# Four units of key and value projection moved ahead of the first attention step, and the rest planned anew

## The chip, the cores and the metric

The kernel runs on one core of one Trainium2 chip. The metric is the time of one execution on the device in microseconds (us). Engines are called PE (matrix products), DVE (vector), ACT (activation), POOL (general) and SP (which here only issues DMAs).

## What is computed

A cross attention over 16 heads of 32 channels, then a feed-forward block. All 1600 query tokens attend to all 5776 context rows. Cut to the part that the change touches:

```python
q = (x @ Wq + bq).reshape(1, B * N, H, hd)          # x: layernorm of (16, 100, 512), H = 16, hd = 32
kv = (cond @ Wkv + bkv).reshape(1, -1, 2, H, hd)    # cond: (16, 361, 512)
k, v = (kv[:, :, 0], kv[:, :, 1])
q, k = _fq_sym(q * scale, axis=-1), _fq_sym(k, axis=-1)   # 8-bit steps, one scale for each row and head
v = _fq_sym(v, axis=2)                                    # one scale for each channel, over all rows
attn = _fq_unsigned(softmax(einsum('bhqd,bhkd->bhqk', q, k)), axis=-1)
out = einsum('bhqk,bhkd->bhqd', attn, v)
```

## The kernel before, in words

The context rows are cut into NU = 46 tiles of 128 rows. The heads are taken in NG = 4 groups of four. One **unit** (g, u) projects context tile u onto the keys and the values of head group g: `unit` on PE (lines 562 to 587; eight fp32 products and a bias product for it, in four slices), `unit_out` on ACT (lines 804 to 818; a key half and a value half, PSUM to SBUF, which counts up `s_kve`), and `load_unit` on SP (line 324), which loads the context tile into one of RING = 4 buffers CT and first waits until PE has done the unit four before it (`s_ku`). Four units are a batch: DVE reduces it (`batch`), ACT rounds it one step later (`k_round`) and splits it two steps later (`k_high`), POOL does `k_scale` and `k_parts`, SP stores it three steps later (`store_k`).

The **first stage** runs all 46 units of group 0, with the query tiles between them: 9 behind the first nine batches, and tiles 9 to 12 behind the last. Then ACT turns all values of group 0 into integers (`value_ints`, three parts, lines 855 to 863), and SP transposes them in the DMA engines (lines 477 to 481).

The **attention loop** has NA = 200 steps. A step is one tile of 128 query rows of one head against all keys: PE makes the scores in four chunks (`scores`, line 637) into two PSUM buffers PS that take turns; DVE scales each chunk and keeps its least value (line 1119), and closes the step with line 1141; ACT takes the exponential of the step (line 946); SP transposes its result by DMA (line 522); POOL widens it (`unpack`, line 1368); PE multiplies it by the values four steps later (`values`, line 656), and ACT takes that product out (`values_out`, line 902). The DMA issues of a step, its transposes with them, all stand in SP's one queue: tiles CT, stores of key batches, stores of finished heads (`store_out`, at step 7 of each 25), the key pieces of the next head (`load_head`, at 1, 3, 5, 6, 8, 15, 16, 18, 20 and 22 of each 25), then the transpose.

The units of groups 1 to 3 are woven into these steps. `plan_units` (lines 98 to 106) gives each its step: a group starts seven steps after the end of the one before, and has one unit in each step, with two in the step in which u // 6 (group 1) or u // 16 (groups 2 and 3) grows. `UNITS` is the same table by step. A unit's four slices stand on PE behind the four chunks of scores and values; `unit_out` stands on ACT one step ahead in its loop, between the exponential and `values_out`. The attention loop on PE thus begins with the first chunk of scores of step 0 and a slice of unit (1, 0) behind it, at a point where ACT is at `value_ints`.

Of the kernel before, what the change touches and what calls it, by code (L numbers as in the profile page):

```python
# [44 lines left out]
NT = -(-TOK // P)  # L45
LAST = TOK - (NT - 1) * P
FULL = NT - 1
NU = -(-KEYS // P)
# [12 lines left out]
VT_LO = (0, 16, 32)  # L61
# [10 lines left out]
NB = 4  # L72
# [25 lines left out]
def plan_units():  # L98


    steps, start = {}, 0
    for g in range(1, NG):
        for u in range(NU):
            steps[g, u] = start + u - (u // 16 if g > 1 else u // 6)
        start = steps[g, NU - 1] + 7
    return steps

# [2 lines left out]
UNITS = {}  # L110
# [31 lines left out]
def build(nc, x, ctxt, ctxl, Wq, bq, Wkv, bkv, Wp, bp, w13T, w2T, norm_w, eye, Qd, Kd, Od, Rd, out):  # L142
    ctx = ExitStack()
    with ctx:
# [132 lines left out]
        M = {n: sem(n) for n in names}  # L277
# [46 lines left out]
        def _(sp):  # L324
# [100 lines left out]
                                   Qd[0:Q_HEAD * P, 0, :]).then_inc(M["s_q0"], 16)  # L425
            store_k(0, NBT - 3)
            load_wg(1)
            for s in range(3):
                for g, u in UNITS[s]:
                    load_unit(g, u)  # L430
            store_k(0, NBT - 2)
            store_q(Q_HEAD)
            load_head(0, 3)
# [48 lines left out]
            sp.wait_ge(M["s_qd0"], 16 * (-(-NT // 2)))  # L482
            sp.wait_ge(M["s_qd1"], 16 * (NT // 2))
            load_head(0, 0)
            for i in range(NA):
                p, j = divmod(i, PAIRT)
                for g, u in UNITS.get(i + 3, []):
# [39 lines left out]
            for s in range(NT + 3):  # L527
                if s < NT:
                    n = rows(s)
# [14 lines left out]
                if 0 <= s - 1 < NT:  # L544
                    t = s - 1
                    n = rows(t)
# [4 lines left out]
                if 0 <= s - 3 < NT:  # L551
                    t = s - 3
                    n = rows(t)
# [7 lines left out]
        def _(pe):  # L561
# [47 lines left out]
            for b in range(NBT):  # L609
                for u in BATCH[b]:  # L610
                    unit(0, u)
                if b == 0:
                    pe.wait_ge(M["s_bk"], 16 * 2)
                    x_transpose(0)
                for t in Q_AFTER[b]:
                    query(t)
                    if t + 1 < NT:
                        x_transpose(t + 1)
            def scores(i, c):

                n = NC_ * i + c
                _, segs = tile_of(i)
                if c == 0:
                    for h, *_r in segs:
                        pe.wait_ge(s_kt[h % 3], 16 * NC_ * (h // 3 + 1))
                        if h == 0 and i < Q_HEAD:
                            pe.wait_ge(M["s_q0"], 16)
                        else:
                            pe.wait_ge(s_qt[h % 3], 16 * (h // 3 + 1))
                if n == 1:  # L630
                    pe.wait_ge(M["s_qe"], NT)
                if n >= 2:
                    pe.wait_ge(M["s_ev"], n - 1)
                for f in range(0, CW[c], 512):
                    w = min(512, CW[c] - f)
                    for h, q0, r, p0 in segs:
                        last = pe.matmul(PS[n % 2][p0:p0 + r, f:f + w], QT[h % 3][0:PARTS * HD, q0:q0 + r],  # L637
                                         KT[h % 3][0:PARTS * HD, c * CHUNK + f:c * CHUNK + f + w],
                                         start=True, stop=True)
                last.then_inc(M["s_qk"], 1)  # L640

            def values(i, part):

                _, segs = tile_of(i)
                g = i // PHASE
# [3 lines left out]
                if part == 0:  # L649
                    if i % PHASE == 0:  # L650
                        for r in range(VRING if g else 0):
                            pe.wait_ge(s_vb[r], 16 * (NBT * g // VRING))
                        pe.wait_ge(M["s_vi"], 16 * len(VT_LO))
                    pe.wait_ge(*((M["s_pve"], i) if i else (M["s_kve"], NU)))
                for u in range(*PV_PART[part:part + 2]):
                    last = pe.matmul(PO[:, 0:w], PT[i % 2][:, u, :].bitcast(F16),  # L656
                                     VI[g % 2][:, u, h * HD:h * HD + w], start=(u == 0), stop=(u == NU - 1))
# [144 lines left out]
        def _(act):  # L802
# [118 lines left out]
                    act.wait_ge(M[f"r_st{t % 2}"], 16 * (t // 2))  # L921
                act.activation(XO[t % 2][0:n, :], PK[0:n, :], ACT.Copy).then_inc(M["r_xo"], 1)

            for u in UNITS[0]:
                unit_out(*u)
            def transposed(t):
                act.wait_ge(M["f_tp"], t + 1)
# [10 lines left out]
            for i in range(NA):  # L938
                act.wait_ge(M["s_mx"], i + 1)
                if i < 2:  # L940
                    act.wait_ge(M["s_pad"], i + 1)
                if i == 0:
                    act.wait_ge(M["s_vt"], len(VT_LO))
                if i >= 2:
                    act.wait_ge(s_tr[i % 2], 16 * (i // 2))
                act.activation(Pr[i % 2].rearrange("p t q b -> p t b q"),  # L946
# [513 lines left out]
```

## Time and profile before

| | us |
|---|---|
| median of 3 runs | 1908.86 |
| lowest and highest of them | 1904.17, 1917.34 |
| the profiled execution | 1917.34 |
| its span in the trace | 1915.5 |

The profiled execution is the slowest of the three; 1.84 us of its time lie outside the span. All durations below are from it. A view of windows gives, for each stretch, its length, the busy time and count of each engine, the granted clock of PE as a share of 2.4 GHz, the DMA engines' share and GB/s. In a view of waits a row names who waited, for whom, the sum, how often, and the longest.

### The profile page before, as it was taken

How to read it: one execution, taken by the hardware profiler on the slowest of the kernel's cores; microseconds unless marked ns; L12 is line 12 of the kernel's file. 1: busy time of each engine (PE TensorE's matmuls, PEld its weight loads, DVE VectorE, ACT ScalarE, POOL GpSimd, SP SyncE). 2: the span in 40 equal slices, each digit the busy share in tenths (PEclk: the TensorE clock that was granted, in tenths of full speed). 3: DMA queues.
4: the chain of work that ended last, by engine and by line, in shares of the span. 5: the costliest groups of instructions: out<-in, count | busy, mean ns of one | idle time of the engine just before them, and what ended most of it. 6: DMA issues, size and time to landing. Idle time of an engine off the chain costs nothing.

```text
span 1915.5 us, 40494 instructions
## 1 busy us (share of the span) xinstructions
PE 1668.9 (87%) x16216; PEld 1133.2 (59%) x16216; DVE 1697.5 (89%) x2665; ACT 1372.3 (72%) x1324; POOL 1450.2 (76%) x1166
## 2 busy tenths in 40 slices
PE   7997988888988888888888888898878888779998
PEld 6884666655556656645666566444445545358776
DVE  6769999989999999999989999999989989876665
ACT  2447898988788888887788888877778778632322
POOL 1342889888998988989988889999997887732332
PEclk9999999998799999967999999655788989789999
DMA  5668889896999889969997999787979977742221
GB/s 175 218 202 200 173 165 206 176 200 129 190 173 207 163 179 195 188 129 193 170 194 155 193 177 191 133 167 148 184 150 168 199 162 143 150 109 50 65 56 45
DMA packets 851482, 309.87 MB, mean 162 GB/s; under 512 B 784928, under 2 KB 813920, under 8 KB 851168
## 3 DMA queue, kind: packets, MB, share of 16 engines
q1 hardware_dynamic: 851296, 307.29, 78.1%
q8 instruction: 129, 2.11, 0.4%
q14 instruction: 57, 0.47, 0.1%
HBM read 74.25 MB, written 39.58 MB: 59 GB/s over the span
## 4 chain that ended last, share of the span: by engine, by line
DVE 31%; PE 26%; issue 14%; POOL 13%; DMA 9%; ACT 5%; SPq 2%; POOLq 0%; DVEq 0%; ACTq 0%
DVE S L1119 27%; POOL PT L1368 10%; DMA PP<-Pr 7%; PE PS L741 5%; PE PS L637 5%; PE PK L578 3%; PE PK L792 3%; PE PS L605 2%; ACT Pr L946 2%; PE PO L656 2%; PE PK L580 2%; PE PK L679 1%; PE PO L580 1%; SPq L522 1%; PE PO L578 1%
## 5 line engine op out<-in xcount | busy, mean ns | idle before, releaser
L1119 DVE TENSOR_SCALAR_CACHE_REDUCE S<-PS,SQN 128x1536 f32<-128x1536 f32 (+1 forms) x768 | 1286.9, 1714 | 63.7 <-PE PS L637 50.7
L1368 POOL CAST PT<-PP 128x1536 uint16<-128x1536 uint8 (+1 forms) x800 | 1103.6, 1424 | 124.7 <-DMA PP<-Pr 122.2
L946 ACT ACTIVATE Pr<-S,MS 128x5888 uint8<-128x5888 f32 x200 | 1041.8, 5209 | 217.9 <-DVE MJ L1141 145.1
L637 PE MATMUL PS<-KT,QT 96*128 96x512 bf16 (+1 forms) x2496 | 726.7, 418 | 127.4 <-DVE S L1119 115.7
L656 PEld LDWEIGHTS PO<-VI,PT 128*128 128x128 f16 x9200 | 350.9, 99 | 318.6 <-issue 160.1
L656 PE MATMUL PO<-VI,PT 128*128 128x32 bf16 x9200 | 366.9, 181 | 78.6 <-ACT AO L902 66.6
L637 PEld LDWEIGHTS PS<-KT,QT 96*128 96x128 bf16 (+1 forms) x2496 | 211.4, 105 | 339.4 <-issue 162.7
L578 PE MATMUL PK<-WG,CT 128*128 128x128 f32 (+1 forms) x1288 | 221.6, 303 | 6.0 <-DMA CT<-ctxt 5.4
L580 PE MATMUL PK<-CT,WG 128*128 128x128 f32 (+1 forms) x1288 | 212.9, 294 | 0.0
L578 PEld LDWEIGHTS PK<-WG,CT 128*128 128x128 f32 (+1 forms) x1288 | 174.2, 199 | 8.3 <-issue 7.0
L580 PEld LDWEIGHTS PK<-CT,WG 128*128 128x128 f32 x1288 | 168.0, 194 | 1.7 <-issue 0.6
L741 PE MATMUL PS<-W,XIF 128*128 128x512 f32 (+3 forms) x624 | 142.8, 386 | 10.4 <-issue 6.3
L741 PEld LDWEIGHTS PS<-W,XIF 128*128 128x128 f32 (+1 forms) x624 | 113.9, 188 | 40.7 <-POOL XIF L1411 10.0
L1271 POOL TENSOR_TENSOR KB<-KB,kam 128x512 f32<-128x512 f32 (+1 forms) x48 | 48.6, 1014 | 95.6 <-DVE kam L1040 95.6
L1283 POOL TENSOR_TENSOR KD<-KE,kam 128x512 f32<-128x512 f32 (+1 forms) x48 | 48.6, 1013 | 59.9 <-ACT KE L829 59.9
L816 ACT ACTIVATE KB<-PK 128x128 f32<-128x128 f32 (+1 forms) x161 | 43.5, 270 | 62.6 <-PE PK L580 62.0
L991 ACT ACTIVATE TG<-G 128x1408 f32<-128x1408 f32 (+1 forms) x13 | 18.0, 1384 | 77.0 <-DVE G L1206 77.0
L1206 DVE SCALAR_TENSOR_TENSOR G<-PS,sc,TG 128x1408 f32<-128x1408 f32 (+1 forms) x13 | 21.9, 1683 | 57.4 <-PE PS L741 57.4
L792 PE MATMUL PK<-W,IQF 128*128 128x512 f32 (+1 forms) x286 | 68.1, 393 | 4.6 <-POOL IQF L1417 1.8
L1422 POOL TENSOR_SCALAR GW<-GW,sc 128x1408 f32<-128x1408 f32 (+1 forms) x13 | 18.6, 1434 | 69.5 <-DVE sc L1227 69.5
L679 PE MATMUL PK<-WP,OT 128*128 128x256 f32 (+1 forms) x168 | 65.6, 483 | 0.0
L1119 DVE DVE_READ_ACCUMULATOR S<-PS,SQN 128x1 f32 x768 | 64.5, 84 | 0.0
(154 smaller groups left out, 1441.5 us busy)
## 6 DMA issues: line engine op xcount, KB each, us to landing
CT<-ctxt SPq DMA_DIRECT2D x180, 256.0 KB, 3.3
k_rows<-KS SPq DMA_DIRECT2D x44, 512.0 KB, 4.3
q_rows<-QS SPq DMA_DIRECT2D x13, 512.0 KB, 4.2
W13F<-w13T SPq DMA_DIRECT2D x12, 352.0 KB, 3.7
PP<-Pr SPq DMA_TRANSPOSE x200, 6.0
XT<-x SPq DMA_DIRECT2D x12, 256.0 KB, 3.3
XR<-x SPq DMA_DIRECT2D x12, 256.0 KB, 3.4
base_rows<-XO SPq DMA_DIRECT2D x12, 256.0 KB, 3.4
```

The costliest lines, as they stand in the source:

```text
L578: pe.matmul(bank[0:n, 0:GC], CT[k % RING][:, d, 0:n], WG[:, d, 0, :], start=(d == 0), stop=False)
L580: last = pe.matmul(bank[:, GC:GC + n], WG[:, d, 1, :], CT[k % RING][:, d, 0:n], start=(d == 0), stop=(d == NK - 1))
L637: last = pe.matmul(PS[n % 2][p0:p0 + r, f:f + w], QT[h % 3][0:PARTS * HD, q0:q0 + r], KT[h % 3][0:PARTS * HD, c * CHUNK + f:c * CHUNK + f ...
L656: last = pe.matmul(PO[:, 0:w], PT[i % 2][:, u, :].bitcast(F16), VI[g % 2][:, u, h * HD:h * HD + w], start=(u == 0), stop=(u == NU - 1))
L679: pe.matmul(PK[0:n, cols], OT[:, k, half:half + n], WP[:, k, cols], start=(k == 0 and half == 0), stop=False)
L741: last = pe.matmul(PS[half][0:n, f:f + w], XF[:, c, 0:n], W13[:, c, a, half * FF + f:half * FF + f + w], start=(c == 0 and a == 0), stop=( ...
L792: last = pe.matmul(PK[0:n, :], IQF[t % 2][:, k, 0:n], W2[:, k, a, :], start=(k == 0 and a == 0), stop=(k == NF - 1 and a == WPARTS - 1))
L946: act.activation(Pr[i % 2].rearrange("p t q b -> p t b q"), S[i % 2].rearrange("p (t b q) -> p t b q", b=2, q=P), ACT.Exp, bias=MS[:, i % ...
L1119: v.tensor_scalar(S[i % 2][:, c * CHUNK:c * CHUNK + CW[c]], PS[n % 2][:, 0:CW[c]], neg_step, None, ALU.mult, ALU.min, accum_out=MN[:, i % ...
L1271: gp.tensor_tensor(KA, KA, kam[:, kb % 2, 1, 0:m].unsqueeze(2).to_broadcast([P, m, HD]), ALU.mult).then_inc(M["s_kn"], 1)
L1283: gp.tensor_tensor(v3(KD), v3(KE), kam[:, kb % 2, 0, 0:m].unsqueeze(2).to_broadcast([P, m, HD]), ALU.mult).then_inc(M["s_k6"], 1)
L1368: gp.tensor_copy(PT[i % 2][:, 2 * t0:2 * t1, :].rearrange("p (t b) q -> p t b q", b=2), PP[i % 2][:, t0:t1, :].bitcast(U8).rearrange("p t ...
```

## The change

Three things are changed in the table of steps, and what follows from them in the queues.

- Group 1: its first four units (NB = 4) get step -1. PE does them whole, behind the last query tile and ahead of all scores, into the banks PK and PO in turn; ACT takes them out behind `value_ints`, ahead of the loop. The other 42 units start at step 0, with two in a step where (u - 4) // 7 grows: 5 steps with two units (6, 12, 18, 24, 30) where there were 7 (5, 10, 15, 20, 25, 30, 35). The group ends at step 36 where it ended at 38.
- Groups 2 and 3: one unit a step. Before, group 2 ran from step 45 to 88 with two in 60 and 75, and group 3 from 95 to 138 with two in 110 and 125. Now group 2 runs from 43 to 88 and group 3 from 95 to 140.
- SP loads the four tiles of step -1 where it loaded the first three units; the tiles of steps 0 to 2 are loaded behind the transposes of the values and the queries of head 0.

Two waits are gone: PE's on all queries at the second chunk of scores, and ACT's on its own `value_ints` at the first exponential. The first product with the values now waits for NU + NB units.

```diff
@@ plan_units
-            steps[g, u] = start + u - (u // 16 if g > 1 else u // 6)
+            steps[g, u] = start + u if g > 1 else -1 if u < NB else u - NB - (u - NB) // 7
@@ sync, end of the first stage
             load_wg(1)
-            for s in range(3):
-                for g, u in UNITS[s]:
-                    load_unit(g, u)
+            for u in UNITS[-1]:
+                load_unit(*u)
             store_k(0, NBT - 2)
@@ sync, ahead of the loop
             load_head(0, 0)
+            for s in range(3):
+                for g, u in UNITS[s]:
+                    load_unit(g, u)
             for i in range(NA):
@@ tensor, behind the last query tile
+            for u in UNITS[-1]:
+                unit(*u)
+
             def scores(i, c):
...
-                if n == 1:
-                    pe.wait_ge(M["s_qe"], NT)
...
-                    pe.wait_ge(*((M["s_pve"], i) if i else (M["s_kve"], NU)))
+                    pe.wait_ge(*((M["s_pve"], i) if i else (M["s_kve"], NU + NB)))
@@ scalar
-            for u in UNITS[0]:
+            for u in UNITS[-1] + UNITS[0]:
                 unit_out(*u)
...
-                if i == 0:
-                    act.wait_ge(M["s_vt"], len(VT_LO))
```

**PE at the start of the loop.** Before, behind the last query tile (L605) the first chunk of scores (L637) follows at once:

```order
L605 MATMUL PS<-WQ,XNT 128x512 x4
L637 MATMUL PS<-KT,QT 128x512 x3
L578 MATMUL PK<-WG,CT 128x128 x2
L637 MATMUL PS<-KT,QT 128x512 x3
L578 MATMUL PK<-WG,CT 128x128 x2
```

Now (lines 607, 640, 580 and 582 are the same as 605, 637, 578 and 580 before):

```order
L607 MATMUL PS<-WQ,XNT 128x512 x4
L580 MATMUL PK<-WG,CT 128x128 x4
...
L582 MATMUL PO<-CT,WG 128x128 x4
L580 MATMUL PK<-WG,CT 128x128 x4
...
L582 MATMUL PO<-CT,WG 128x128 x4
L640 MATMUL PS<-KT,QT 128x512 x3
L580 MATMUL PK<-WG,CT 128x128 x2
L640 MATMUL PS<-KT,QT 128x512 x3
```

Four whole units, (1, 0) to (1, 3), stand ahead of the first scores, and the slice of a unit behind these now belongs to unit (1, 4).

**SP at the same place.** Before, behind the last two stores of queries (L392) come the transposes of the values (L480), the queries of head 0 (L376), and one tile CT (L330), that of step 3, ahead of the first transpose of the loop (L522):

```order
L392 DMA q_rows<-QS 128x2048 x2
L480 DMA_TRANSPOSE VI<-VI 128x16x128 x2
L480 DMA_TRANSPOSE VI<-VI 128x14x128
L376 DMA_TRANSPOSE QT<-q_rows 128x1x512
L330 DMA CT<-ctxt 128x512
L522 DMA_TRANSPOSE PP<-Pr 128x23x128
```

Now the tiles of steps 0 to 3 stand there, (1, 4) first:

```order
L392 DMA q_rows<-QS 128x2048 x2
L479 DMA_TRANSPOSE VI<-VI 128x16x128 x2
L479 DMA_TRANSPOSE VI<-VI 128x14x128
L376 DMA_TRANSPOSE QT<-q_rows 128x1x512
L330 DMA CT<-ctxt 128x512 x4
L524 DMA_TRANSPOSE PP<-Pr 128x23x128
```

**ACT between the exponentials of steps 59 and 60.** Before, the step in which a batch is rounded (L824, L829) has two units to take out (L816, L818), since step 60 has two:

```order
L946 ACTIVATE Pr,ZB<-S,MS 128x23x2x128
L824 ACTIVATE KI<-KB 128x512
L829 ACTIVATE KE<-KI 128x512
L816 ACTIVATE KB<-PK 128x4x32
L818 ACTIVATE VV<-PK,BV 128x128
L816 ACTIVATE KB<-PK 128x4x32
L818 ACTIVATE VV<-PK,BV 128x128
L902 ACTIVATE AO<-PO 128x32
L946 ACTIVATE Pr,ZB<-S,MS 128x23x2x128
```

Now there is one unit and no rounding (lines 947, 819, 821 and 905 are 946, 816, 818 and 902 before):

```order
L947 ACTIVATE Pr,ZB<-S,MS 128x23x2x128
L819 ACTIVATE KB<-PK 128x4x32
L821 ACTIVATE VV<-PK,BV 128x128
L905 ACTIVATE AO<-PO 128x32
L947 ACTIVATE Pr,ZB<-S,MS 128x23x2x128
```

The rounding of this batch stands two steps earlier now, with one unit beside it.

## Rows read from the trace of the kernel before

**Rows 1.** The page, part 1: busy us, share of the span, instructions.
```profile
PE 1668.9 (87%) x16216; PEld 1133.2 (59%) x16216; DVE 1697.5 (89%) x2665; ACT 1372.3 (72%) x1324; POOL 1450.2 (76%) x1166
```

**Rows 2.** Waits of DVE, 165 to 1261 us (steps 0 to 144).
```profile
DVE S L1119 <- PE PS L637: 38.9, 68, 3.2
```

**Rows 3.** Windows of single steps, from one L1141 to the next.
```profile
179.13:185.93 6.80, 5.50 (x33) 3.72 (x33) 6.77 (x10) 5.72 (x4) 1.80 (x2) 1.00 0.98 200
...
207.72:214.57 6.85, 6.39 (x79) 4.58 (x78) 6.82 (x10) 5.81 (x5) 6.62 (x6) 1.00 0.76 164
243.97:251.55 7.58, 6.46 (x77) 4.36 (x75) 6.91 (x10) 7.21 (x11) 7.42 (x7) 1.00 0.70 165
281.90:288.91 7.01, 6.53 (x89) 4.93 (x90) 6.91 (x11) 6.12 (x7) 7.01 (x7) 1.00 0.83 174
...
392.63:400.80 8.17, 6.46 (x77) 4.36 (x75) 6.91 (x10) 8.13 (x13) 7.32 (x8) 1.00 1.05 203
...
621.01:629.23 8.22, 6.46 (x77) 4.36 (x75) 6.91 (x10) 8.18 (x13) 7.47 (x7) 1.00 0.77 175
...
997.62:1007.62 10.00, 8.24 (x90) 5.52 (x88) 7.00 (x11) 8.69 (x14) 8.82 (x8) 0.83 0.51 105
...
422.62:436.36 13.74, 9.41 (x92) 7.30 (x92) 8.19 (x13) 10.99 (x15) 12.48 (x11) 0.75 0.78 157
651.05:660.59 9.54, 8.23 (x91) 6.23 (x92) 8.13 (x14) 7.75 (x11) 8.91 (x8) 0.82 0.59 109
...
591.96:599.16 7.20, 6.10 (x75) 4.36 (x75) 6.85 (x10) 7.15 (x10) 7.04 (x6) 1.00 1.09 193
599.16:607.33 8.17, 6.88 (x91) 5.22 (x92) 8.04 (x13) 5.92 (x5) 8.17 (x7) 1.00 0.68 147
```

**Rows 4.** Timeline of PE in step 31: start, us, what, [idle before, releaser].
```profile
394.17 0.45 PE L656 MATMUL PO<-VI,PT 128*128 128x32 bf16 x12 [1.17 <-ACT AO L902]
```

**Rows 5.** Timeline of ACT: ahead of that, and in step 33.
```profile
391.81 0.62 ACT L824 ACTIVATE KI<-KB 128x512 int8<-128x512 f32 x1
...
393.81 0.22 ACT L902 ACTIVATE AO<-PO 128x32 f32<-128x32 f32 x1
...
419.71 5.21 ACT L946 ACTIVATE Pr<-S,MS 128x5888 uint8<-128x5888 f32 x1 [4.48 <-DMA PP<-Pr]
```

**Rows 6.** Timeline of PE, start of the loop.
```profile
160.92 0.81 PE L637 MATMUL PS<-KT,QT 96*128 96x512 bf16 x3
...
167.55 1.28 PE L637 MATMUL PS<-KT,QT 96*128 96x512 bf16 x3 [4.22 <-DVE S L1119]
```

**Rows 7.** Timeline of DVE there.
```profile
164.40 0.96 DVE L1090 TENSOR_SCALAR QS<-QF 128x1536 bf16<-128x1536 f32 x1
...
165.67 1.82 DVE L1119 TENSOR_SCALAR_CACHE_REDUCE S<-PS,SQN 128x1536 f32<-128x1536 f32 x1
...
167.41 1.81 DVE L1119 TENSOR_SCALAR_CACHE_REDUCE S<-PS,SQN 128x1536 f32<-128x1536 f32 x1
```

**Rows 8.** Timeline of ACT there.
```profile
166.71 1.70 ACT L863 ACTIVATE VI<-Pr 128x1792 bf16<-128x1792 int8 x1
```

**Rows 9.** Timeline of PE, two units of the first stage.
```profile
110.43 1.06 PE L578 MATMUL PK<-WG,CT 128*128 128x128 f32 x8
...
112.33 1.06 PE L578 MATMUL PO<-WG,CT 128*128 128x128 f32 x8
```

**Rows 10.** Timeline of SP, start of the loop.
```profile
165.76 7.51 SPq L480 DMA_TRANSPOSE VI<-VI  x3
173.37 1.72 SPq L376 DMA_TRANSPOSE QT<-q_rows  x1
175.13 0.58 SPq L330 DMA_DIRECT2D CT<-ctxt  x1
```

**Rows 11.** Line 330, 175 to 176 us: issue to landing.
```profile
DMA to landing us min/median/max: 3.0/3.0/3.0
```

**Rows 12.** Window at the start of the loop.
```profile
165.00:170.00 5.00, 2.45 (x9) 1.63 (x10) 4.93 (x8) 3.37 (x2) 0.00 (x0) 0.78 0.82 200
```

## The prediction

> **What bounds the kernel now.** I read the page's busy shares first: DVE is busy for 89% of the span and PE for 87% [rows 1], so neither alone explains the time. The steps of the attention loop do. I cut the loop at the end of each step (line 1141) and asked for the windows. A plain step lasts 6.80 us and DVE is busy for 6.77 of them; a step in which DVE also reduces a batch lasts 8.17 with 8.04 busy [rows 3]. The loop is thus bound by DVE, and 144 steps and 36 batches at this pace are a floor that no plan of units can change. What a plan can change is the time in which DVE waits. From step 0 to step 144 it waits 38.9 us for PE's scores, in 68 places [rows 2]. The steps that the change touches are among the longer ones. Behind a step with two units a step lasts 6.85, 7.58, 7.01, 8.17, 8.22 or 10.00 us [rows 3], in place of 6.80. The reader is to see that it isn't PE's own work: in step 31 (8.17 us) PE is busy for only 6.46 us and ACT for 8.13 [rows 3]. PE waits 1.17 us for ACT's line 902 [rows 4], because ACT first rounds a batch and takes out two units; from the rounding to line 902 it needs 393.81 - 391.81 = 2.00 us [rows 5]. The wait passes from ACT to PE to DVE.
>
> **The loop, part by part: what the new plan saves.** The eleven steps behind a double step cost, above 6.80: in group 1 0.05, 0.78, 0.21 and 1.37, and three that repeat the 7.58 and the 7.01 (0.78, 0.30 and 0.31), together 3.8; in groups 2 and 3 1.42 and 3.20 and two like the first (1.5 and 1.3), together 7.4. That is 11.2 us [rows 3]. What decides is what ACT has beside the second unit: rounding a batch costs 0.78 to 1.4, splitting one 0.2 to 0.3, nothing 0.05. In the new plan five double steps are left (6, 12, 18, 24, 30). ACT takes their units out in 5, 11, 17, 23 and 29, and rounds in 2, 6, 9, 13, 16, 20, 23, 27 and 30: one meets a rounding, one (17) a splitting. I take 3 x 0.05 + 0.25 + 0.9 = 1.3. In groups 2 and 3 the rounding now meets a single unit. Step 57 is such a step, 7.20 us, so 0.40 stays at each of the four places [rows 3], 1.6 together. Saved: 11.2 - 1.3 - 1.6 = 8.3.
>
> Second, batches of groups 2 and 3 came three steps apart behind a double step (62 and 65, 77 and 80, and twice in group 3), where the delay of one batch fell on the reduction of the next: step 65 lasts 9.54 us, 1.37 above its 8.17 [rows 3]. Now they are four apart everywhere. At 0.4 in place of 1.1 to 1.4, three of the four times, this is 2.4 us; I take it with bounds 0 and 4.
>
> Third, step 35, the dearest: 13.74 us, 5.57 above a batch step, with PE's clock at 0.75 [rows 3]. Its exponential two steps before had waited 4.48 us for a DMA transpose [rows 5]. SP had, in steps 31 and 32, a store of keys and a key piece, then two tiles and the store of heads. In the new plan the store of keys moves to step 32 and one of the two tiles goes. In the old plan the same arrangement stands at step 57, which lasts 7.20. I take half of the 5.57, 2.6, with bounds 0 and 5.5; the queue stays crowded, and the same crowd may meet elsewhere.
>
> The sum of the loop is 8.3 + 2.4 + 2.6 = 13.3 saved, between 5 (half of the first term and nothing else) and 20 (all three at their upper ends, with the two double steps of group 1 that still meet ACT's batches at nothing).
>
> **What the new start costs.** This is the part that speaks against the change. Before, PE begins the scores at 160.92 [rows 6], and its second chunk then waits for DVE, which ends the queries at 164.40 + 0.96 and takes chunk 0 at 165.67 and chunk 1 at 167.41 [rows 7]. So PE had about 4 us to spare (its idle stretch of 4.22 [rows 6]), and four units at 112.33 - 110.43 = 1.90 each [rows 9] need 7.6. That alone would be 3.6 us late. But unit (1, 2) uses PK again, so it waits for ACT's `unit_out` of (1, 0), which stands behind `value_ints`, and that ends at 166.71 + 1.70 = 168.41 [rows 8]. Add 0.4 for the copy (the 2.00 us of [rows 5] less two instructions of 0.62 are two of them): PE goes on at 168.8, ends (1, 3) at 172.6, and has chunk 0 of the scores at 173.4. DVE starts 173.4 - 165.67 = 7.7 late.
>
> Behind chunk 0 stands the first slice of unit (1, 4), and its tile is now loaded behind the value transposes and the queries of head 0. The old kernel issued a tile at that very place, at 175.13 [rows 10], landing 3.0 later [rows 11]: 178.1. The slice and 0.81 of scores follow, so DVE takes chunk 1 at about 179.2 in place of 167.41: 11.8 late. Steps 0 to 3 had no excess before, their units were hidden at 6.80 us a step, so nothing is given back there. PE stands still from 164.8 to 168.8 and from 173.4 to 178.1. In the stretch of the old idle time the granted clock was 0.78 [rows 12] and a chunk took 1.28 in place of 0.81 [rows 6], while DVE went on without a gap [rows 7]; I add 0.4 and take 12.2. The bounds: 7.7 if the tile is no obstacle, and 15 if it lands 3 us later, as it shares the queue with three transposes of 7.51 us of issue [rows 10].
>
> The Trainium skill (TensorE: Matmul & The Clock Gate, section "HAM oscillation — how this bites in real kernels") warns that waits for data between groups of matmuls throttle the array again, each time. The trace agrees in the clock (0.78, [rows 12]). By the rule both new stretches would be paid for. The first is covered by the tile's landing; behind the second, scores and slices at the lower level would hold DVE up by about 1 us, and the sum would be 12.8 in place of 12.2.
>
> **The waits removed.** PE's wait on all queries ended before ACT's copies would let PE go on, and ACT's wait is on its own earlier instruction. Both at nothing. The later due dates of group 3 (140 for 138) leave its last batch ready for step 150 as before; two steps more have a unit. Nothing, between -1 and +1.
>
> **The sum.** 12.2 - 13.3 = -1.1 on the 1917.34 us of the profiled execution, 1916.2. That execution lies 8.5 above the median of the runs, and what I move are differences, so for the median it is 1908.86 - 1.1 = 1907.8, rounded to 1908: no change that can be measured.
>
> **Rivals.** (a) The start is hidden. For it: DVE is the bound and two PSUM buffers lie between. Against it: PE's order holds all scores behind four units, and ACT's behind `value_ints`. The time would be 1908.86 - 13.3 = 1895.6. (b) The start costs all of it and the loop gives back little, since the waits are DMA's and ACT's more than the second unit's. For it: the wait of 4.48 on a DMA transpose [rows 5], and step 57, which has one unit's rounding and still costs 0.40 [rows 3]. With 15 late at the start and 4 saved: 1919.9. It decides from the point where less is saved than the 12.2. (c) The crowd on SP's queue meets anew: batches and key pieces change their places, and a few steps like 35 arise at 5.57 each [rows 3]. Four of them in place of one, with 8.3 saved and 12.2 late: 1908.86 + 3.9 + 16.7 = 1929.5. Against it: in groups 2 and 3 fewer stores now meet a key piece (counted from the tables of steps, 10 for 18).
>
> **How the numbers follow.** The forecast has 0.70, (a) 0.13, (b) 0.12, (c) 0.05. The three runs of before lie 13 us apart, so about 1% (19 us) is what a measurement tells from no change. The forecast's own range is 12.2 - 20 to 15 - 5, or 1901 to 1919. (a) and (b) widen it to 1896 and 1920. Faster by over 1% needs (a) with the upper bound of the savings, 1908.86 - 20: 0.06. Slower by over 1% is (c): 0.05. The rest, 0.89, is within 1%.
>
> **What the profile after would show.** Right: no scores on PE before 168 us; L1119 first near 173.4, a gap ahead of its second until about 179; the first L1141 12 us later than before; steps 61, 76, 111 and 126 near 7.2 us; the wait of DVE for PE's scores in the loop some 8 to 12 us smaller. The forecast is wrong if chunk 1 starts before 175 (then (a)), if step 65 or 80 stays above 9 us (then (b)), or if any step not next to 35 passes 12 us (then (c)).

## The result: 0.55% slower, just outside the range

| | before | after |
|---|---|---|
| median of 8 runs | 1909.62 | 1923.15 |
| lowest and highest | 1902.25, 1917.34 | 1914.78, 1931.31 |
| the profiled execution | 1917.34 | 1914.62 |
| its span | 1915.5 | 1912.7 |

The ratio is 1.0055, with an interval from 1.0032 to 1.0079: 10.5 us slower, between 6.1 and 15.1. (It rests on more executions than the eight of the table, whose medians lie 13.5 apart: on record are 31 of after, with a median of 1920.73.) That is still "within 1%" by the bound of the prediction, but the median of 1923.15 lies above its upper end of 1920, and the sign of the sum was wrong.

The two profiled executions say the opposite: the one of after is 2.8 us shorter than that of before. The one of before was the slowest of its eight runs, the one of after was faster than all eight of its own. So both kernels were profiled again (runs b0 and a0 below), and every reading of the loop in this text rests on several profiles.

The page of after, part 1, beside [rows 1]:

```profile
PE 1661.8 (87%) x16216; PEld 1129.8 (59%) x16216; DVE 1696.9 (89%) x2665; ACT 1372.0 (72%) x1324; POOL 1447.2 (76%) x1166
```

The instructions are the same in number and the busy time too: only their order and their waits differ.

**The start of the loop.** The timeline of PE in after, where [rows 6] shows before (start, us, what, [idle before, releaser]):

```profile
164.66 1.11 PE L582 MATMUL PO<-CT,WG 128*128 128x128 f32 x8
...
169.88 1.90 PE L580 MATMUL PK<-WG,CT 128*128 128x128 f32 x8 [4.10 <-ACT VV L821]
171.68 1.96 PE L582 MATMUL PK<-CT,WG 128*128 128x128 f32 x8
173.47 1.05 PE L580 MATMUL PO<-WG,CT 128*128 128x128 f32 x8
...
175.37 0.81 PE L640 MATMUL PS<-KT,QT 96*128 96x512 bf16 x3
...
179.12 0.71 PE L580 MATMUL PK<-WG,CT 128*128 128x128 f32 x4 [2.94 <-DMA CT<-ctxt]
179.67 0.89 PE L640 MATMUL PS<-KT,QT 96*128 96x512 bf16 x3
```

PE stands still twice: 4.10 us ahead of unit (1, 2) for ACT, and 2.94 us ahead of the first slice of (1, 4) for its tile. ACT and SP in after at the same place, beside [rows 8] and [rows 10]:

```profile
167.61 1.70 ACT L866 ACTIVATE VI<-Pr 128x1792 bf16<-128x1792 int8 x1
169.21 0.26 ACT L819 ACTIVATE KB<-PK 128x128 f32<-128x128 f32 x1
169.37 0.36 ACT L821 ACTIVATE VV<-PK,BV 128x128 f32<-128x128 f32 x1
```

```profile
166.66 7.60 SPq L479 DMA_TRANSPOSE VI<-VI  x3
174.36 1.75 SPq L376 DMA_TRANSPOSE QT<-q_rows  x1
176.15 2.00 SPq L330 DMA_DIRECT2D CT<-ctxt  x4
```

And the timeline of DVE, which starts chunk 0 at 176.32 where it was 165.67 and chunk 1 at 180.60 where it was 167.41 [rows 7]; the last row closes step 0:

```profile
176.32 1.82 DVE L1120 TENSOR_SCALAR_CACHE_REDUCE S<-PS,SQN 128x1536 f32<-128x1536 f32 x1 [9.79 <-PE PS L640]
...
180.60 1.82 DVE L1120 TENSOR_SCALAR_CACHE_REDUCE S<-PS,SQN 128x1536 f32<-128x1536 f32 x1 [2.46 <-PE PS L640]
...
182.84 1.82 DVE L1120 TENSOR_SCALAR_CACHE_REDUCE S<-PS,SQN 128x1536 f32<-128x1536 f32 x1 [0.41 <-PE PS L640]
...
186.06 0.16 DVE L1142 TENSOR_SCALAR_CACHE_REDUCE MJ<-MN 128x4 f32<-128x4 f32 x1
```

**The loop.** The waits of DVE for the scores up to step 144, beside [rows 2] (waited for, sum, times, longest):

```profile
DVE S L1120 <- PE PS L640: 44.0, 61, 9.8
```

9.79 of the 44.0 are the first chunk, so some 34 are left for the rest, for 38.9 before. Windows of the former double steps and their neighbours in after (steps 59, 61, 76, 79, 111, 126 and 134), beside [rows 3]: length, busy PE, PEld, DVE, ACT, POOL, then the granted clock as a share of 2.4 GHz, DMA share, GB/s:

```profile
616.28:624.78 8.50, 7.86 (x88) 5.74 (x88) 6.94 (x11) 7.23 (x10) 8.34 (x7) 0.80 1.05 227
632.94:639.80 6.86, 6.12 (x76) 4.23 (x75) 6.82 (x11) 5.80 (x5) 4.58 (x5) 1.00 0.94 166
740.75:748.92 8.17, 6.87 (x91) 5.22 (x92) 8.04 (x14) 5.92 (x5) 7.58 (x7) 1.00 0.74 115
762.57:771.27 8.70, 7.88 (x88) 5.59 (x88) 7.16 (x11) 7.53 (x11) 8.54 (x8) 0.80 0.84 177
997.84:1008.49 10.65, 8.78 (x75) 6.11 (x75) 7.00 (x10) 8.45 (x12) 9.39 (x9) 0.68 0.49 98
1113.51:1120.31 6.80, 5.85 (x63) 3.70 (x61) 6.76 (x11) 6.57 (x6) 4.18 (x5) 1.00 0.95 150
1171.96:1181.45 9.49, 7.72 (x88) 5.58 (x88) 6.92 (x11) 8.53 (x12) 8.60 (x7) 0.82 1.16 224
```

Steps 61 and 126 are cheap now. But steps 59, 79 and 111, each with one unit and the rounding of a batch, cost 1.70, 1.90 and 3.85 above 6.80, where the prediction had 0.40 (step 57 in [rows 3]). Step 134, with one unit and no rounding, costs 2.69, and had no term at all.

### The profile page after: what moved, and what is told of

It reads as the page before. It is cut to its first block, busy times and chain, and to the rows that moved or that the text cites. A ratio compares the mean times of both kernels' runs of the same rounds, so it can differ in the third digit from the quotient of the medians.

```text
span 1912.7 us, 40494 instructions
## 1 busy us (share of the span) xinstructions
PE 1661.8 (87%) x16216; PEld 1129.8 (59%) x16216; DVE 1696.9 (89%) x2665; ACT 1372.0 (72%) x1324; POOL 1447.2 (76%) x1166
## 4 chain that ended last, share of the span: by engine, by line
DVE 36%; PE 23%; POOL 15%; issue 13%; DMA 6%; ACT 5%; SPq 2%; POOLq 0%; DVEq 0%; ACTq 0%
DVE S L1120 32%; POOL PT L1369 11%; PE PS L744 5%; DMA PP<-Pr 4%; PE PS L640 4%; PE PK L580 3%; PE PK L795 3%; PE PS L607 2%; ACT Pr L947 2%; PE PO L659 1%; PE PK L582 1%; POOL VV L1304 1%; PE PO L582 1%; PE PO L580 1%; DVE kam L1034 1%
## 5 line engine op out<-in xcount | busy, mean ns | idle before, releaser
L640 PE MATMUL PS<-KT,QT 96*128 96x512 bf16 (+1 forms) x2496 | 719.0, 413 | 130.4 <-DVE S L1120 117.9
L580 PE MATMUL PK<-WG,CT 128*128 128x128 f32 (+1 forms) x1272 | 220.6, 303 | 13.1 <-DMA CT<-ctxt 8.1
L580 PEld LDWEIGHTS PK<-WG,CT 128*128 128x128 f32 (+1 forms) x1272 | 172.9, 199 | 16.4 <-issue 11.8
L795 PEld LDWEIGHTS PK<-W,IQF 128*128 128x128 f32 (+1 forms) x286 | 51.6, 184 | 19.3 <-issue 5.3
```

The source lines that it names most:

```text
L580: pe.matmul(bank[0:n, 0:GC], CT[k % RING][:, d, 0:n], WG[:, d, 0, :], start=(d == 0), stop=False)
L795: last = pe.matmul(PK[0:n, :], IQF[t % 2][:, k, 0:n], W2[:, k, a, :], start=(k == 0 and a == 0), stop=(k == NF - 1 and a == WPARTS - 1))
```

## The experiments

All profiles are read in the same way, since one step by itself proves little. "First end" is where step 0 closes. The first stage ends up to 3.4 us earlier or later, whatever is changed behind it (the last query product ends at 161.08 in before, 163.41 in b0, 161.99 in after, 164.09 in e3), so "start" counts from the end of that product to the first end. The **excess** of a stretch of steps is the time between its closing rows, less 6.80 for each step and 1.37 more for each with a batch reduced. "New" and "old" name the tables of steps of groups 1 and of 2 and 3; for after over the whole loop, 1469.8 - 199 x 6.80 - 36 x 1.37 = 67.3, which is the sum of its four excesses.

| kernel | front | tables | first end | start | excess of steps 1-45 | 46-95 | 96-145 | 146-199 | ratio to before |
|---|---|---|---|---|---|---|---|---|---|
| before | old | old, old | 172.36 | 11.28 | 15.7 | 16.0 | 21.6 | 30.8 | 1 |
| b0 | old | old, old | 174.68 | 11.27 | 9.9 | 15.4 | 17.6 | 27.9 | 1.0012 |
| after | new | new, new | 186.06 | 24.07 | 10.0 | 13.5 | 18.0 | 25.7 | 1.0055 |
| a0 | new | new, new | 185.95 | 23.9 | 10.3 | 13.7 | 18.7 | 29.1 | 1.0056 |
| e1 | old | old, single | 172.7 | 11.28 | 12.9 | 19.7 | 27.4 | 38.8 | 1.0098 |
| e2 | new | new, old | 185.5 | 24.4 | 11.8 | 13.4 | 17.0 | 27.7 | 1.0072 |
| s1 | ACT early | new, new | 186.8 | 25.1 | 9.1 | 12.6 | 16.1 | 29.3 | 1.0061 |
| s2 | tiles early | new, new | 182.9 | 22.1 | 11.3 | 13.1 | 21.5 | 31.0 | 1.0066 |
| s3 | both early | new, new | 176.7 | 16.0 | 10.5 | 13.0 | 15.8 | 30.6 | 1.0002 |
| e3 | both early | new, old | 180.1 | 16.0 | 11.6 | 15.8 | 21.6 | 22.8 | 1.0014 |
| s4 | two units | mended, new | 174.4 | 11.27 | 25.4 | 14.1 | 18.2 | 26.2 | 1.0073 |
| s5 | two units | mended, new | 173.8 | 11.27 | 9.1 | 13.9 | 17.9 | 28.7 | 0.9987 |
| s5 again | two units | mended, new | 172.2 | 11.27 | 10.0 | 15.0 | 19.1 | 31.3 | 0.9983 |
| s7 | four, spread | new, new | 173.3 | 11.28 | 10.9 | 13.6 | 19.6 | 33.2 | 0.9989 |
| n1 | old | 9 doubles, new | 173.1 | 11.28 | 22.3 | 16.0 | 16.6 | 31.2 | 1.0048 |
| n2 | old | 9 doubles, new | 173.4 | 11.27 | 15.2 | 10.9 | 17.7 | 26.4 | 1.0010 |

**Both kernels again (b0, a0)**, no edit.

> The kernel before, unchanged: a second profile of it. Every theory expects the median of before, 1909 us, within 4 us. What is open is where its loop stands: the profiled execution of before was its slowest of eight, so theory L (the loop of the old plan was measured too slow in that one profile) expects this one to last less than the 1486.6 us from the first to the last L1141 of the loop, by 5 to 10 us, while theory S (the profiles are fair, and something outside of the loop explains the result) expects 1486 within 3.

> The changed kernel, unchanged: a second profile. All theories expect a ratio of about 1.005 to 1.007. The profiled execution of after was the fastest of its eight. Theory L expects its loop, from the first to the last L1141, at 1475 to 1482 us in place of 1469.8, so that the start (12.8 us late) is the whole loss and the loop saves 3 to 8. Theory S expects 1470 within 3.

Ratios 1.0012 [0.9989, 1.0035] and 1.0056 [1.0036, 1.0076]: the loss is real. The loop from the first end to the last takes 1486.6 us in before and 1473.3 in b0, 13.3 less, and 1469.8 in after and 1474.4 in a0: the first pair of profiles has the new loop 16.8 shorter, the second 1.1 longer. By the table, two executions of the same kernel differ by 5.8 in steps 1 to 45. Three steps of b0 (35, 65 and 80), which the prediction had priced from before at 13.74, 9.54 and 9.27:

```profile
424.40:433.02 8.62, 7.78 (x92) 6.19 (x92) 8.13 (x14) 7.64 (x12) 8.32 (x7) 1.00 0.92 203
...
647.95:656.12 8.17, 6.70 (x91) 5.23 (x92) 8.04 (x14) 7.13 (x10) 8.01 (x7) 1.00 0.61 126
...
759.16:767.33 8.17, 6.70 (x90) 5.05 (x91) 8.04 (x14) 7.36 (x10) 7.95 (x7) 1.00 0.62 128
```

The same program, and all three are gone or nearly so (a batch step has 8.17 by itself). They are not gone for good: e1, which has the old table of group 1, has 12.21 at step 35, and e3, which has the old tables of groups 2 and 3, has 10.25 at step 80.

```profile
421.79:434.00 12.21, 9.31 (x92) 7.20 (x92) 8.19 (x13) 9.68 (x15) 10.95 (x9) 0.86 0.86 180
```

And in b0 DVE waits for the scores for 31.5 us in all, for 38.9 in before:

```profile
DVE S L1119 <- PE PS L637: 31.5, 63, 2.2
```

**Groups 2 and 3 alone, one unit a step, with the old start (e1)**

```diff
-            steps[g, u] = start + u - (u // 16 if g > 1 else u // 6)
-        start = steps[g, NU - 1] + 7
+            steps[g, u] = start + u - (0 if g > 1 else u // 6)
+        start = steps[g, NU - 1] + (7 if g == 1 else 6)
```

> The kernel before with one unit a step in groups 2 and 3 alone (steps 45 to 90 and 96 to 141); group 1 and the start as before. If the plan of groups 2 and 3 saves what I forecast (7.4 - 1.6 + 2.4 = 8 us), 1901 us, ratio 0.996. If what it saves is taken back by other waits (theory W), 1909 to 1912, ratio 1.000 to 1.001.

Ratio 1.0098 [1.0066, 1.0130], 18.7 us slower: a miss, and a confounded one. With group 1 still ending at 38, group 3 ends at 141, one step later than in after, and its values come late for the head that begins at 150. The window of step 154, and PE's wait in it:

```profile
1324.78:1345.80 21.02, 5.97 (x70) 3.27 (x70) 7.03 (x11) 6.68 (x7) 19.69 (x20) 0.59 0.63 124
```

```profile
1338.93 0.48 PE L656 MATMUL PO<-VI,PT 128*128 128x32 bf16 x12 [14.59 <-DMA VI<-VB]
```

The 14.2 us of this step are put down to ending one step too late; neither before (138) nor after (140) has such a step, but the last step of group 3 was not varied by itself. They are not the whole: steps 46 to 145 have 47.0 of excess, 12 more than with the old tables. The same one unit a step, placed two steps later than in after in group 2 and one later in group 3, is dearer than the plan with double steps. The comparison was then made anew from the other side.

**The other way round: after with the old tables of groups 2 and 3 (e2)**

```diff
-            steps[g, u] = start + u if g > 1 else -1 if u < NB else u - NB - (u - NB) // 7
-        start = steps[g, NU - 1] + 7
+            steps[g, u] = start + u - u // 16 if g > 1 else -1 if u < NB else u - NB - (u - NB) // 7
+        start = steps[g, NU - 1] + (9 if g == 1 else 7)
```

> The changed kernel with the old plan for groups 2 and 3 (steps 45 to 88 and 95 to 138); start and group 1 as changed. If the new plan of groups 2 and 3 saves 8 us, this is 8 us slower than the changed kernel: ratio to before 1.010 or so. If it saves nothing (theory W), the ratio is that of the changed kernel, 1.006.

Ratio 1.0072 [1.0044, 1.0099]. Against a0's 1.0056 the single units are worth 0.0016, or 3 us; the prediction had 8.2 for them. The intervals overlap.

**The start: ACT's copies earlier (s1)**

```diff
+                if n == 2:
+                    for u in UNITS[-1][:2]:
+                        unit_out(*u)
-            for u in UNITS[-1] + UNITS[0]:
+            for u in UNITS[-1][2:] + UNITS[0]:
```

The first two lines stand in ACT's loop over the parts of `value_ints`, ahead of its third part.

> The changed kernel; ACT takes out units (1, 0) and (1, 1) between the second and the third part of the integer values instead of behind all three. Theory T (the whole loss is the late start, and at the start the tile of unit (1, 4) decides): chunk 0 is 4 to 5 us late in place of 9.8, but chunk 1 still waits for the tile, so the first L1142 stays within 1.5 us of 186 and the ratio stays at 1.005. Rival A (ACT's copies decide): first L1142 near 180, ratio 1.002. Rival G (the loss is in the loop's plan): ratio 1.0056 whatever the start does.

Ratio 1.0061 [1.0041, 1.0081]. The first wait went, and the second took all of it. DVE and PE in s1:

```profile
171.03 1.82 DVE L1123 TENSOR_SCALAR_CACHE_REDUCE S<-PS,SQN 128x1536 f32<-128x1536 f32 x1 [4.75 <-PE PS L640]
...
181.33 1.82 DVE L1123 TENSOR_SCALAR_CACHE_REDUCE S<-PS,SQN 128x1536 f32<-128x1536 f32 x1 [8.48 <-PE PS L640]
```

```profile
178.79 1.23 PE L580 MATMUL PK<-WG,CT 128*128 128x128 f32 x4 [7.89 <-DMA CT<-ctxt]
```

Chunk 0 comes 5.29 earlier than in after, chunk 1 0.73 later: it still waits for the tile, now 7.89 us in place of 2.94.

**The start: the tiles earlier (s2)**, and **both (s3)**, which is s1 and s2 together

```diff
+            for s in range(2):
+                for g, u in UNITS[s]:
+                    load_unit(g, u)
...
-            for s in range(3):
-                for g, u in UNITS[s]:
-                    load_unit(g, u)
+            for g, u in UNITS[2]:
+                load_unit(g, u)
```

The added loop stands ahead of the value transposes; the other place is behind `load_head(0, 0)`.

> The changed kernel; SP loads the tiles of steps 0 and 1 ahead of the value transposes instead of behind them and the queries. Theory T: chunk 0 is as late as in the changed kernel (176), chunk 1 follows at once, at 178 in place of 180.6, first L1142 near 183.5, ratio 1.004. Rival A: the same, since ACT's copies decide then. Rival G: ratio 1.0056.

> The changed kernel with both: ACT's copies between, tiles early. Theory T: chunk 0 at 171, chunk 1 at 173, first L1142 near 178.5, that is 7.5 us less than the changed kernel and 4 to 6 more than before: ratio 1.0015 to 1.002. Rival G: 1.0056 with a first L1142 of 178.5, the gain being lost in the loop. If the transposes of the values, now issued later, hold the loop up, step 4 is long.

s2: 1.0066 [1.0049, 1.0084]; s3: 1.0002 [0.9988, 1.0017]. In s2 the first wait stays whole:

```profile
168.60 2.04 PE L582 MATMUL PK<-WG,CT 128*128 128x128 f32 x8 [4.10 <-ACT VV L823]
```

Its chunk 0 comes at 176.17, as in after, and chunk 1 right behind at 177.91; the first step closes 3.2 earlier. Of these, 1.3 are the first stage, which ended at 160.72 for 161.99; the start itself is 1.9 shorter (22.1 for 24.0). The ratio doesn't show it, which was a miss of the expectation, but 1.9 us lie within the interval. In s3 DVE has

```profile
170.01 1.82 DVE L1125 TENSOR_SCALAR_CACHE_REDUCE S<-PS,SQN 128x1536 f32<-128x1536 f32 x1 [4.74 <-PE PS L642]
...
171.75 1.81 DVE L1125 TENSOR_SCALAR_CACHE_REDUCE S<-PS,SQN 128x1536 f32<-128x1536 f32 x1
```

and 0.0054 of a0's ratio of 1.0056, 10 us, are back. The two waits stand in series ahead of the same chunk: taking away either one gives nothing that can be measured, taking away both gives nearly the whole loss. What is left is 4.7 us of start (16.0 for 11.28): PE's four units themselves less the idle time of before, which the prediction had put at 3.6.

**The old tables of groups 2 and 3 on the mended start (e3)**: s3 with the edit of e2.

> s3_both with the old plan for groups 2 and 3 (45 to 88 and 95 to 138). With s3_both at 1.0002: if the new plan of groups 2 and 3 saves the 8 us of my forecast, 1.0044; by theory C 0.9995 to 1.0015.

1.0014 [0.9996, 1.0032], for s3's 1.0002: 2.3 us for the single units, the same size and sign as from e2, and again with intervals that overlap. e3's first end lies 3.4 behind s3's because its first stage ended 3.4 later (164.09 for 160.72); the start is the same 16.0.

**Two units ahead in place of four (s4, s5)**. PE has 4 us to spare, which two units of 1.9 fill. ACT takes them out where s1 does, the tiles of steps -1 to 1 are loaded at the old place, and the two waits that after removed are put back. The first added line is s4's, the second s5's:

```diff
-            steps[g, u] = start + u if g > 1 else -1 if u < NB else u - NB - (u - NB) // 7
+            steps[g, u] = start + u if g > 1 else -1 if u < 2 else u - 2 - (u - 2) // 6
+            steps[g, u] = start + u if g > 1 else -1 if u < 2 else u - 2 - u // 6
```

> Two units ahead of the loop in place of four (they fit in the 4.22 us in which PE stood idle), both taken out by ACT between the second and the third part of the values; the four tiles at the old place now hold units 0 to 3; group 1 with seven double steps, ending at 36; groups 2 and 3 as in the changed kernel; the two waits that were removed are back. Theory T: the first L1144 or so within 1.5 us of before (172 to 175), so what is left is the loop's saving of 2 to 5 us: ratio 0.998 to 0.9995. Rival G: ratio 1.004 or more.

> s4_two_front with its double steps of group 1 at 3, 8, 13, ... 33 in place of 4, 10, ... 36: the last two batches of group 1 are two steps apart again and not one. In s4 step 42 (6.99 us of excess) and step 45 (5.73) had ACT and POOL wait for the store of the batch before. Theory: both go, the first 45 steps have 10 to 13 us of excess in place of 25.4, ratio 0.998 to 1.000. If the ratio stays at 1.007, it is the two front units and not the spacing of the batches.

> The same kernel as s5_two_front_b, again on another chip, since its 0.9987 (0.9971 to 1.0002) did not part it from no change. If the new table with a start that costs nothing is worth the 2 to 4 us that the profiles show, 0.998 to 0.999 again.

s4: 1.0073 [1.0060, 1.0086], though its start is good (chunk 0 at 167.76, chunk 1 at 169.51). Its step 42 lasts 13.79 and step 45 12.53. The window of step 42, and ACT in it:

```profile
480.71:494.50 13.79, 5.94 (x59) 2.71 (x58) 6.91 (x10) 6.18 (x6) 8.76 (x9) 0.59 0.58 144
```

```profile
485.55 0.42 ACT L846 ACTIVATE KS<-KD 128x256 bf16<-128x256 bf16 x1 [6.36 <-DMA k_rows<-KS]
```

By the table the last two batches of group 1 are complete one step apart (units 43 and 45 in steps 35 and 36), and ACT's splitting of the second waits for the store of the one before. s5 shifts the doubles so that they are two apart, as in after (34 and 36); its step 42, in the profile of the repeat:

```profile
476.10:483.12 7.02, 6.52 (x60) 3.25 (x59) 6.82 (x10) 5.41 (x3) 6.86 (x8) 0.50 1.08 242
```

s5: 0.9987 [0.9971, 1.0002], and once more 0.9983 [0.9961, 1.0005]. Twice below one, each interval just reaching it. The start is 11.27 us in s4 and in both profiles of s5, as in before: the two units cost it nothing.

**Four units ahead, spread (s7)**: two of them in PE's idle time ahead of query tile 11, two behind the last; ACT takes the first two out at once, the others as in s1; tiles early; the two waits back.

```diff
+                    if t == NT - 3:
+                        for u in UNITS[-1][:2]:
+                            unit(*u)
-            for u in UNITS[-1]:
+            for u in UNITS[-1][2:]:
                 unit(*u)
```

> The changed kernel's table with its four front units spread over the idle stretches of PE: units (1, 0) and (1, 1) in the 3.4 us ahead of the third last query product, (1, 2) and (1, 3) behind the last; ACT takes the first two out before the values and the other two between their second and third part; the tiles of steps 0 to 2 are loaded ahead of the value transposes. Theory T: the first L1141-like row at 172 to 175 as before, all of the start's 12.8 us recovered, and the loop's small saving is left: ratio 0.997 to 0.999. If the ratio is 1.001 or more, the new table saves nothing in the loop even with its own start.

0.9989 [0.9973, 1.0005], chunk 0 at 166.61. The query product behind this idle time in after, and the units and the same product in s7:

```profile
151.79 5.37 PE L607 MATMUL PS<-WQ,XNT 128*128 128x512 f32 x8 [3.38 <-DVE QF L1081]
```

```profile
149.70 1.16 PE L582 MATMUL PK<-WG,CT 128*128 128x128 f32 x8 [1.45 <-DMA CT<-ctxt]
...
153.60 3.60 PE L609 MATMUL PS<-WQ,XNT 128*128 128x512 f32 x8
```

The two units start in the idle time and push the product from 151.79 to 153.60, but it takes 3.60 in place of 5.37 and ends at 157.2 in both: they cost nothing. The whole start is 11.28 us, so all four units are hidden.

**The old start with the new tables (n1, n2)**, so that nothing is ahead of the scores and group 1 ends at 36 all the same, with nine double steps; the first added line is n1's, the second n2's:

```diff
-            steps[g, u] = start + u - (u // 16 if g > 1 else u // 6)
+            steps[g, u] = start + u - (0 if g > 1 else u // 5)
+            steps[g, u] = start + u - (0 if g > 1 else (u + 4) // 5)
```

> The kernel before with its start, group 1 in steps 0 to 36 (nine double steps), and groups 2 and 3 as in the changed kernel (43 to 88 and 95 to 140, one unit a step). My forecast's terms (0.4 to 1.4 us a double step, 8 us for groups 2 and 3): two doubles more in group 1 at about 0.5 each, so 7 us faster, ratio 0.996. Theory C (the excess of a step comes from a rounding that meets a late transpose, not from the second unit, so that the table matters little): ratio 0.999 to 1.001.

> The kernel before with its start; group 1 ends at 36 with nine double steps (0, 4, 8, ... 32), so that its last two batches stay two steps apart; groups 2 and 3 as in the changed kernel. It is n1_old_start_new_table without the crowd at steps 42 and 45 (7.17 and 5.53 us of excess there). If the new table of groups 2 and 3 is worth the 8 us of my forecast less 1 to 3 for the two more doubles, 0.997 or less. By theory C (the tables are worth 0 to 4 us) 0.999 to 1.001, with 10 to 14 us of excess in steps 1 to 45.

n1: 1.0048 [1.0026, 1.0069], with 7.2 and 5.5 above their due in steps 42 and 45, the same last batches one step apart as in s4. n2, with these two apart: 1.0010 [0.9990, 1.0030]. It has the new tables of groups 2 and 3 and more double steps in group 1 (excess 15.2, of which 4.6 at step 45), and is no faster than before.

## Why the prediction was wrong

**The start (forecast 12.2 late): right in mechanism and size.** Step 0 closes at 186.06 and 185.95, for 172.36 and 174.68: 12.5 late in the mean, and 12.7 late counted from the end of the first stage (24.07 and 23.9 for 11.28 and 11.27). No scores before 168 (175.37 was the first). DVE's first chunk was to come at 173.4 and came at 176.32, the second at 179.2 and came at 180.60. Of the 2.9 that the first chunk was later than forecast, 0.9 had come with the first stage (PE's first unit starts at 161.82, where before had its scores at 160.92). The rest is mostly the lower clock at which the units ran behind the first of the two waits, and which the forecast of 173.4 had left out: ahead of (1, 2) PE was idle for 4.10 us, and the window behind, in after, has the granted clock at 0.66, a mixture of 1.2 and 2.4 GHz, for 1.00 in the one ahead, and the one behind the second idle stretch has 0.66 too:

```profile
165.00:170.00 5.00, 0.90 (x8) 0.74 (x8) 1.46 (x4) 4.97 (x7) 0.00 (x0) 1.00 0.61 160
170.00:175.00 5.00, 5.00 (x31) 4.93 (x32) 0.00 (x0) 0.70 (x3) 0.00 (x0) 0.66 1.07 199
...
180.00:185.00 5.00, 4.91 (x23) 3.42 (x21) 3.98 (x5) 0.24 (x2) 0.00 (x0) 0.66 0.14 52
```

The halves of (1, 2) take 1.90 and 1.96 where 1.06 is usual [rows 9]. Half of the 2.9 us was hidden behind the tile (PE starts its slice at 179.12; the forecast had it landing at 178.1); DVE's gap of 0.41 ahead of its third chunk is what the second idle stretch cost. The Trainium skill (TensorE: Matmul & The Clock Gate, section "HAM oscillation — how this bites in real kernels") describes a kernel whose array is throttled again behind each wait for data between its groups of matmuls. This trace agrees, with 0.66 behind each of the two stretches. The extra 1 us that the prediction had drawn from it stood apart from the sum, and 0.41 of it was found.

**The loop (forecast 13.3 saved, some 5 found): this step failed.** The term that failed is the first, 8.3 for the double steps, and with it the assumption that nothing new arises elsewhere. The other two terms held.

I compare means over profiles, and leave out s4 and n1 in the steps that their last batches spoilt, and plans that have a table of their own (e1's groups 2 and 3, group 1 of s5 and n2). Steps 46 to 145 have 37.6, 33.0, 30.4 and 37.4 of excess with the old tables (before, b0, e2, e3), 34.6 in the mean, and 31.7 over the eleven profiles with the new (28.6 to 34.6): 2.9 saved where the terms 7.4 - 1.6 + 2.4 said 8.2. (With e1's 47.0 among the new it would be 1.6.) Steps 1 to 45: 12.8 (before, b0, e1) and 10.7 (the eight with the new table), 2.1 saved where 3.8 - 1.3 + 2.6 said 5.1. Together 5.0, and 12.7 - 5.0 = 7.7 us slower, inside the measured 6.1 to 15.1. The single profiles overlap, so 5.0 is a rough figure. The times say rather less: the paired ratios (e2 against a0, e3 against s3) give 3 and 2.3 us for groups 2 and 3, and where the start is known, after's 12.7 less 10.5, s7's 0 and 2.1 faster, and s3's 4.7 less 0.4 leave 2.2, 2.1 and 4.3 for the whole loop. Term by term:

- *Step 35, 2.6 saved: held.* With the old table of group 1 the step has 5.57, 0.45 and 4.05 of excess (before, b0, e1), 3.4 in the mean, and the exponential waits 4.48, 3.53 and 2.98 for a DMA transpose near it. In all eight profiles with the new table it has 0.02.
- *Batches three apart, 2.4 saved: held.* Steps 65, 80, 115 and 130 together have 3.62, 2.18, 0.94 and 3.52 with the old tables, 2.6 in the mean. The batch steps that took their place (64, 80, 116, 132) have none in all eleven profiles.
- *Double steps, 8.3 saved: failed.* The cost of those removed was real. In group 1 the seven steps behind a double had 3.6 to 3.8 together in each of three profiles, and in groups 2 and 3 steps 61, 76, 111 and 126 had 6.7 in the mean of four, where the prediction had 7.4. What failed is what was to stay. In group 1 the steps behind the five doubles that are left (7, 13, 19, 25, 31) take 2.7 for the 1.3 put down, and step 18, itself a double step, has 1.15 in all eight where no term stood. In groups 2 and 3 0.40 was to stay at each of four places. But in the mean of the eleven, steps 59 and 79 have 1.5 each, where the four with the old tables have 0.1, and step 111 has 2.8, where with its second unit it had 2.6: taking the unit away gave nothing there.

The 0.40 came from one row, step 57, in one execution; with the same old tables that step took 7.67, 8.77 and 8.45 in b0, e2 and e3. Step 59 shows that it was only the lower of two prices. The same wait of PE, in after and in s1:

```profile
616.82 0.45 PE L659 MATMUL PO<-VI,PT 128*128 128x32 bf16 x12 [0.97 <-ACT AO L905]
```

```profile
616.44 0.45 PE L659 MATMUL PO<-VI,PT 128*128 128x32 bf16 x12 [0.97 <-ACT AO L908]
```

In after the step lasts 8.50 with the granted clock at 0.80 (its window is shown above), and in s1:

```profile
615.90:623.07 7.17, 6.10 (x75) 4.36 (x75) 6.85 (x10) 7.13 (x10) 7.01 (x6) 1.00 1.10 256
```

So the 0.40 (0.37 here) holds at the full clock, in three of the eleven profiles; in the other eight the clock falls and the step costs 1.7 or more. What decides between the two no run shows. Step 111 is another case:

```profile
999.63 0.48 PE L659 MATMUL PO<-VI,PT 128*128 128x32 bf16 x12 [2.23 <-ACT AO L905]
```

```profile
992.49 5.21 ACT L947 ACTIVATE Pr<-S,MS 128x5888 uint8<-128x5888 f32 x1 [2.30 <-DMA PP<-Pr]
```

ACT's exponential of this step begins 2.30 late through a DMA transpose, PE waits 2.23 for ACT's copy, and the step runs at a granted clock of 0.68. With the old tables the exponential waits there too, 2.14 to 2.45 us in all four profiles. In a0 the steps 59, 111 and 134 are as dear as in after (9.88, 11.49 and 10.57, the clock at 0.65, 0.70 and 0.68).

Step 134 had no term. There is no rounding in it; its exponential waits for a transpose:

```profile
1167.70 5.21 ACT L947 ACTIVATE Pr<-S,MS 128x5888 uint8<-128x5888 f32 x1 [4.31 <-DMA PP<-Pr]
```

And SP's queue ahead of it, in steps 131 and 132 of after, has the store of a key batch and a key piece, and then a tile and the store of heads:

```profile
1164.78 0.40 SPq L338 DMA_DIRECT2D k_rows<-KS  x1
1165.22 2.70 SPq L386 DMA_TRANSPOSE KT<-k_rows  x1
...
1172.06 0.58 SPq L330 DMA_DIRECT2D CT<-ctxt  x1
1172.68 0.43 SPq L442 DMA_DIRECT2D attn_out<-AO  x1
```

This is the arrangement that the prediction had read in steps 31 and 32 of before, ahead of its step 35. It has moved by a hundred steps. Steps 134 and 135 together have 3.3 of excess in the mean of the eleven (2.2 to 4.3) and 0.2 in the four with the old tables. So steps 61, 76 and 126 and the three-apart batches gave back some 6.6, and 59, 79, 134 and 135 took some 5.9 of it. That the arrangement is the cause is read from the rows, and no run moved it by itself.

**The prediction's own arithmetic** has three slips, none of which decides: half of 5.57 is 2.8 and not 2.6, half of the first term is 4.2 and not 5, and all terms at their upper ends are 19 and not 20.

**Rival (b)**, "the waits are DMA's and ACT's more than the second unit's", with 4 saved, is the closest of the forecasts for the loop (5.0), and its time of 1919.9 the closest to 1923.15. It had 0.12. Its two parts did not both come: its start of 15 late was 12.7. Its sign (step 65 or 80 above 9 us in after) did not show, since they last 6.86 and 8.17; the sign was ill chosen, because the waits came at other steps.

**Rival (c)**, a crowd on SP meeting anew, was right in mechanism at one place, 134, at 2.69 in place of 5.57. Its sign, a step above 12 us, is there by the letter (step 167 of after, 12.05), but tells nothing: it lies behind the last unit, before has 11.16 there and 12.05 at step 186, and in a0 no step passes 12. The experiments made dearer steps (42 in s4 and n1, 154 in e1) by the distance of batches or the end of group 3; one step of e1, 99, was 7.2 above its due, and why was not pursued. **Rival (a)**, a hidden start, fell, and s3 settles it from the other side: where both waits go, 10 us come back.

**The waits removed, and the later due dates: nothing.** s5 and s7 have the waits back and are the fastest. Group 3's end at 140 cost nothing that shows, as forecast, but by e1 the margin is one step. **The check by DVE's wait** (8 to 12 smaller in the loop) was badly chosen: it is 34 in after without the start, 38.9 in before and 31.5 in b0. Its scatter in one kernel is as large as the effect.

What stays open: what makes the clock fall behind the same wait in one execution and not in another; why steps 146 to 199, where after's plan changes nothing, have between 22.8 and 33.2 of excess (38.8 in e1, with its step 154); and some 3 us between the 7.7 of this account and the 10.5 measured, which the interval covers. The best plans, s5 and s7, are 2 to 3 us faster than before by their medians' ratios and about 13 faster than after; that they beat before at all is not quite shown.

## What to carry to other kernels

Before work is put in front of an engine's first dependent step, follow each thing that it needs through the queue in which it stands (here ACT's copies behind `value_ints`, the tile behind three transposes): such waits come in series, and mending one of them shows nothing. And before a term is built on a step's excess, profile the same kernel more than once. Some excesses repeat to 0.01 us (step 18, 1.15 in eight profiles); those with a late transpose or a lowered clock are draws, and want a mean. When the cost of a step is taken away, count what arises at the steps where the moved work now stands: here each of the removed costs was real, and most of it came back elsewhere.

## What was not expected of the hardware

- Single steps of one program differ between executions by far more than the whole does: step 35 took 13.74 and 8.62 us, while the kernel's eight times lie between 1902 and 1917. The granted clock differed with them (0.75 and 1.00).
- Waits of 2.2 us and even 0.97 us within a busy loop stood beside a lowered clock (0.68 in step 111, 0.80 in step 59 of after), not only the 4 us at its start. Behind the same 0.97 us in s1 the clock stayed at 1.00.
- Work put into PE's idle time can make the work behind it shorter: two units in a 3.38 us gap, and the query product behind them takes 3.60 us in place of 5.37 and ends at the same time.
